# Projecting q one iteration earlier, the right sums in y's banks, and x1's column sums taken by ScalarE copies

## The reference, cut to what matters

```python
# layer 0: triangle multiplication
x = _layernorm(pair, ln1_w, ln1_b)
left = sigmoid(x @ left1) * (x @ left2)
right = sigmoid(x @ right1) * (x @ right2)
p = einsum('nsre,nkre->nske', left, right)
p = _layernorm(p, ln2_w, ln2_b)
x1 = pair + einsum('nrse,ez->nsrz', p, out_w) * sigmoid(x @ gate)
...
# layer 1
left = x1 @ W_left + b_left + x1 @ W_eq + b_eq
right_sum = sum(x1 @ W_right + b_right, axis=2, keepdims=True)
out = left * right_sum * sigmoid(x1 @ W_gate + b_gate)
return _layer_norm(out @ W_out + b_out + x1, ln_scale, ln_bias)
```

## Time and profile before

| what | value |
|---|---|
| median of 3 runs | 104.78 us (103.95 to 104.85) |
| the profiled execution, its own time | 103.82 us |
| its span, first to last instruction | 101.9 us |
| busy share of the span: TensorE, VectorE, ScalarE, GpSimd | 78%, 69%, 59%, 52% |
| mean granted TensorE clock | 0.958 |

### The profile page before, as it was taken

How to read it: one execution, slowest core, us unless ns; L and a number is a source line. 1 busy time by engine, 2 the same in 40 slices (tenths; PEclk the granted TensorE clock), 3 DMA queues, 4 the chain that set the end, 5 groups by cost and what they waited for, 6 DMA issues and landing times.

```text
span 101.9 us, 3186 instructions
## 1 busy us (share of the span) xinstructions
PE 79.4 (78%) x1260; PEld 59.5 (58%) x1260; DVE 70.5 (69%) x286; ACT 60.4 (59%) x101; POOL 52.9 (52%) x69
## 2 busy tenths in 40 slices
PE   0997999789999999998894889889898779750000
PEld 0994887667877899644552466757566467640000
DVE  0477697946466800399978799997979897299700
ACT  0643977998776267689259944895429762922000
POOL 5138994899910050008555454089075769946400
PEclk9999999999999999999999999999999999998555
DMA  3999997000000000000000000000000606447996
GB/s 50 193 152 147 144 146 77 13 10 13 0 0 6 3 0 0 0 0 0 0 6 3 3 0 6 0 6 0 6 0 6 103 12 98 66 66 115 145 145 97
DMA packets 34079, 4.68 MB, mean 46 GB/s; under 512 B 33936, under 2 KB 34064, under 8 KB 34064
## 3 DMA queue, kind: packets, MB, share of 16 engines
q1 hardware_dynamic: 32304, 4.10, 32.0%
q10 hardware_dynamic: 1760, 0.38, 2.0%
HBM read 2.38 MB, written 2.10 MB: 44 GB/s over the span
## 4 chain that ended last, share of the span: by engine, by line
PE 37%; DVE 29%; ACT 16%; issue 6%; POOL 5%; DVEq 1%; POOLq 0%
PE bank L831 10%; PE bank L894 7%; DVE x1T L709 7%; PE bank L904 5%; DVE stats L670 4%; PE bank L838 4%; PE bank L816 3%; ACT sig L524 3%; ACT L424 3%; DVE o_a L718 3%; DVE st L724 2%; POOL xc L306 2%; DVE lr L742 2%; DVE stats L591 2%; DVE lr L606 2%
## 5 line engine op out<-in xcount | busy, mean ns | idle before, releaser
L367 POOL TENSOR_TENSOR t_tok<-p_sb,rstd 128x512 f32<-128x512 f32 x7 | 10.2, 1457 | 16.6 <-DVE rstd L676 15.8
L831 PE MATMUL bank<-lr_blk,xnT 64*128 64x256 f32 x128 | 15.6, 388 | 0.7 <-ACT xnT L435 0.7
L606 DVE TENSOR_TENSOR lr<-bank,sig_lr 128x512 f32<-128x512 f32 x16 | 10.9, 683 | 6.4 <-ACT sig_lr L444 6.4
L831 PEld LDWEIGHTS bank<-lr_blk,xnT 64*128 64x128 f32 x128 | 11.8, 186 | 3.2 <-issue 1.2
L670 DVE BATCH_NORM_STATS2 stats<-p_sb 128x6 f32<-128x64 f32 x64 | 8.6, 216 | 6.9 <-ACT p_sb L488 6.9
L376 POOL TENSOR_TENSOR oT<-o_a,rsum 128x512 f32<-128x512 f32 x8 | 8.3, 1044 | 8.5 <-DVE o_a L718 8.5
L444 ACT ACTIVATE sig_lr<-bank 128x512 f32<-128x512 f32 x16 | 9.6, 597 | 3.3 <-PE bank L831 3.1
L591 DVE BATCH_NORM_STATS2 stats<-x_tok 128x6 f32<-128x64 f32 x64 | 8.9, 213 | 1.4 <-DMA x_tok<-in_x 1.3
L396 POOL TENSOR_TENSOR sq<-lr,row_rep 128x512 f32<-128x512 f32 x6 | 8.0, 1336 | 2.6 <-DVE lr L742 1.8
L709 DVE SCALAR_TENSOR_TENSOR x1T<-bank,w_rep,u 128x128 f32<-128x128 f32 x32 | 9.3, 347 | 0.1
L306 POOL TENSOR_TENSOR xc<-x_tok,stats 128x512 f32<-128x512 f32 (+1 forms) x8 | 8.1, 1012 | 1.8 <-DVE stats L591 1.8
(11 more groups left out here) (98 smaller groups left out, 169.7 us busy)
## 6 DMA issues: line engine op xcount, KB each, us to landing
x_tok<-in_x SPq DMA_DIRECT2D x14, 128.0 KB, 4.2
out<-sq SPq DMA_DIRECT2D x7, 256.0 KB, 4.0
x_tok<-in_x SPq DMA_DIRECT2D x3, 64.0 KB, 3.1
w_rep<-in_weights ACTq DMA_DIRECT2D x4, 45.1 KB, 3.2
out<-sq ACTq DMA_DIRECT2D x1, 128.0 KB, 3.2
out<-sq SPq DMA_DIRECT2D x1, 128.0 KB, 4.8
x_tok<-in_x ACTq DMA_DIRECT2D x1, 64.0 KB, 2.7
scale_rep<-in_rows SPq DMA_DIRECT2D x1, 64.0 KB, 8.8
```

What stands on the lines that cost most here:

```text
L367: nc.gpsimd.tensor_tensor(t_tok[:, c % 2], by_token(p_sb[:, :, s]), by_token(rstd[:, 1:2, s]).to_broadcast([P, SPC, CH]), ALU.mult).then_i ...
L606: nc.vector.tensor_tensor(lr[:, :, s].rearrange("p f (b q) -> p b f q", q=GRP), src[:, :, 2 * CH:4 * CH], sig_lr[:, j % 3].rearrange("p (b ...
L831: last = nc.tensor.matmul(dst, xnT[half, c, k * P:(k + 1) * P], lr_blk[half], start=True, stop=True, skip_group_check=True)
```

## The change

TensorE projects q of chunk i in its iteration i, where it did so for chunk i-1, and behind y instead of ahead of layer 1's projections. From chunk 1 on the right sums are written into the spare half of the banks Y and not of Q; since `evacuate_y(c)` and `sums_of_right(c+2)` then read the same banks, `project_sums` of chunk c (c > 1) gives the signal `y_ps` that `evacuate_y(c-2)` waits for, and `sums_of_right(c)` waits for that square (`ysq_ready`). VectorE makes x1 of chunks 1 to 7 in one operation of 512 columns without sums. ScalarE makes the sums: `sum_x1(c)`, four copies of 128 columns that accumulate, for each of the chunks 1 to 7. The groups of the roots and the places where they stand in the loops are changed as well, and so is the order of `gate0`.

```diff
-ROOTS2 = [(0, 2), (2, 4), (4, 6), (6, 8)]
+ROOTS2 = [(0, 2), (2, 5), (5, 8)]
-ROOTS3 = [(0, 1), (1, 4), (4, 5), (5, 6), (6, 7), (7, 8)]
-ROOT3_AT = {4: [0], 7: [1], 9: [2, 3]}
+ROOTS3 = [(0, 1), (1, 3), (3, 4), (4, 6), (6, 7), (7, 8)]
+ROOT3_AT = {5: [0], 7: [1], 8: [2], 9: [3]}
...
+            def sum_x1(c):
+                act.wait_ge(x1_ready, BLK * (c + 1))
+                for j in range(BLK):
+                    last = nc.scalar.activation(x1_again[:, c % 2, j * P:(j + 1) * P], x1T[:, c % 3, j * P:(j + 1) * P],
+                                                ACT.Copy, accum_out=x1_sum[:, c, j:j + 1])
+                last.then_inc(x1_summed, 1)
...
-                if i in ROOT3_AT and i < CHUNKS:
-                    nc.scalar.activation(scratch[:], eps[:], ACT.Sigmoid)
+                if i == 3 or i in ROOT3_AT and i <= CHUNKS:
+                    nc.scalar.activation(scratch[:, i:i + 1], eps[:], ACT.Sigmoid)
...
             def sums_of_right(c):
-                dve.wait_ge(rs_ps, c + 1)
-                if c + 1 < CHUNKS:
-                    dve.wait_ge(q_ps, c + 2)
+                if c < 2:
+                    dve.wait_ge(rs_ps, c + 1)
+                else:
+                    dve.wait_ge(ysq_ready, c - 1)
...
+                if c:
+                    nc.vector.scalar_tensor_tensor(out=x1T[:, c % 3], in0=bank[:, XT], scalar=vec("b_out"),
+                                                   in1=u[:, c % 2], op0=ALU.add, op1=ALU.add).then_inc(x1_ready, BLK)
+                    return
...
             def project_sums(c):
-                pe.wait_ge(x1_ready, BLK * (c + 1))
                 if c:
-                    pe.wait_ge(rs_ready, c)
+                    pe.wait_ge(x1_summed, c)
...
-                last.then_inc(rs_ps, 1)
+                last.then_inc(y_ps if c > 1 else rs_ps, 1)
```

More of the change, by code:

```diff
@@ L401, in _ @@
             for i in range(CHUNKS + 2):
-                if i + 2 < CHUNKS:
+                if i + 2 < CHUNKS and i != 3:
                     normalise2(i + 2)
+                for c in BIAS_FIRST.get(i, []):
+                    bias3(c)
                 if 0 <= i - 2 < CHUNKS:
                     times_right(i - 2)
+                if i == 3:
+                    normalise2(5)
                 for c in BIAS_AT.get(i, []):
                     bias3(c)
-            for c in (3, 5, 6):
+            for c in (5, 6):
                 bias3(c)
@@ L466, in _ @@
                 root1_of(b)
-            nc.scalar.activation(scratch[:], eps[:], ACT.Sigmoid)
+            nc.scalar.activation(scratch[:, 0:1], eps[:], ACT.Sigmoid)
             affine1(4)
@@ L538, in _ @@
                     root2_of(1)
-                    evacuate_tT(1)
-                    root2_of(2)
-                    evacuate_tT(2)
+                    nc.scalar.activation(scratch[:, 1:2], eps[:], ACT.Sigmoid)
+                if i < CHUNKS:
+                    evacuate_tT(i)
+                if i == 1:
+                    gate0(2)
+                    gate0(6)
                 if i == 2:
-                    gate0(2)
-                    gate0(3)
                     act.wait_ge(biases, 3)
@@ L547, in _ @@
                     gate1(i - 2)
-                if i < CHUNKS and i not in (1, 2):
-                    evacuate_tT(i)
                 if i == 2:
-                    for c in range(4, CHUNKS):
+                    gate0(7)
+                if 0 < i - 1 < CHUNKS:
+                    sum_x1(i - 1)
+                if i == 2:
+                    for c in (3, 4, 5):
                         gate0(c)
-                if i == 4:
-                    root2_of(3)
+                if i == 3:
+                    root2_of(2)
                 if i == CHUNKS + 1:
@@ L690, in sums_of_right @@
             def sums_of_right(c):
[L691 to L694 removed]
+                if c < 2:
+                    dve.wait_ge(rs_ps, c + 1)
+                else:
+                    dve.wait_ge(ysq_ready, c - 1)
+                if c == 0:
+                    dve.wait_ge(q_ps, 2)
+                b = sums_bank(c)
+                nc.vector.tensor_scalar(two(rsum[:, c]), bank[:, b:b + 2, HALF:HALF + 2], right_bias[:], None, ALU.add
                                         ).then_inc(rs_ready, 1)
@@ L1040, in _ @@
             transpose_t(0)
[L1041 to L1047, removed]
+            project_q(0)
+            project_gate0(6)
+            transpose_t(1)
+            project_gate0(7)
+            project_sums(0)
+            project_q(1)
+            transpose_x(1)
+            for i in range(2, CHUNKS + 3):
+                if i < CHUNKS:
+                    transpose_t(i)
                 if 0 <= i - 2 < CHUNKS:
                     project_1(i - 2)
[L1050 to L1054, removed]
                 if 0 <= i - 3 < CHUNKS:
```

62 lines of the change are left out of this document (38 added, 24 removed).

## The result

| | before | after |
|---|---|---|
| median of the runs | 104.37 us (103.95 to 104.85, 4 runs) | 108.10 us (108.00 to 108.21, 4 runs) |
| the profiled execution, its own time | 103.82 us | 108.14 us |
| its span | 101.9 us | 106.3 us |
| mean granted TensorE clock | 0.958 | 0.936 |

The changed kernel is slower: ratio 1.0356, 95% interval 1.0294 to 1.0417. The forecast was 108.8, in a range from 105.5 to 112.0. The runs of the kernel before lie near 103.8 us or, with a mean granted clock of 0.944 to 0.948 instead of 0.953 to 0.965, near 104.8, so a median of a few of them depends on how many of either it holds.

A forecast was written before the change was run, and what follows sets the result against it. VectorE and TensorE waiting on each other bound the kernel, 4.48 us per x1; the change puts ScalarE's queue in that ring. Lag +1.0 in the opening, +4.9 at i = 8, +4.0 at the end: 104.8 + 4.0 = 108.8, range 105.5 to 112.0.

The forecast's parts named there:

- ScalarE's queue: ScalarE's copies, table loads, roots and squares in order; outside the wait cycle before, forecast to stand in it after the change.
- the ring: Cycle of waits from x1 to x1: VectorE and TensorE before, 4.48 us; after, through ScalarE's sums, TensorE and the square.
- a, the step of an accumulating copy: Start to start of ScalarE's 128-column accumulating copies: taken at 0.31 us, so 1.24 us a chunk, 28 copies in the path.
- The loads cost their row: Each ScalarE table load costs 1.30 us to the next start, not the skill page's 2.66 per switch.
- Opening, x1(3) at 64.8: ScalarE full until layer 0's last root at 61.1; x1 of chunk 3 at 64.8 instead of 63.78, +1.0.
- i = 4 to 8: Loop iterations followed through ScalarE's queue: lag +0.6 at x1(4), +1.5 at x1(6), +1.9 at x1(7), +4.9 at `o_a(7)`.
- End: root over at 93.15, tail "the same work": Root for chunks 4 and 5 ends at 93.15 instead of 89.16; VectorE's tail behind it unchanged, so end 4.0 later.
- The sum: Whole effect: +4.0 us on the profiled execution, 107.8; with the median 0.96 above that execution, 108.8.
- Cheap copies: First rival: fixed step and read-out hidden, a = 0.12, sum falls by 5.3 to -1.3, 103.5; chance 0.07.
- a free read-out: Second rival: the copies' read-out costs nothing, a = 0.20, +0.9, 105.7, about no change; chance 0.14.
- dear copies: Third rival: a = 0.40 gives +6.5, 111.3; a = 0.49 gives +9.0, 113.8; chance 0.09.
- The fourth: Rival: q still waits for x1, `u` starts 0.5 late, time stays 108.8; chance within the forecast's 0.70.

The follow-up runs named there:

- run 1: Changed kernel with x1's sums back on VectorE in four operations, no ScalarE copies, eleven loads kept: 103.14 us, ratio 0.9877 to the kernel before.
- run 5: Kernel before with only x1 in one VectorE operation and its sums by ScalarE copies, seven loads: 108.02 us, ratio 1.0419.
- run 6: Changed kernel with one accumulating copy of 512 columns per chunk instead of four of 128 (sums not the reference's): 105.19 us, ratio 1.0125.
- run 7: Changed kernel with chunk 3's root joined to the group at i = 7, nine loads instead of eleven: 107.22 us, ratio 1.0326.
- run 4: Changed kernel with 16 further identity products on TensorE filling gaps in the last iterations: 108.08 us, ratio 1.0353.
- run 8: Changed kernel with x1's sums back on VectorE and nine loads (edits of run 1 and run 7): 103.13 us, ratio 0.9923.
- run 9: run 8's kernel with GpSimd's products with the right sums moved ahead of the scales and biases: 104.25 us, ratio 0.9997 to the kernel before.
- run 10: Kernel before with the output of chunks 0 to 5 not stored, two stores instead of eight: 102.97 us.
- run 11: run 1's kernel with the output of chunks 0 to 5 not stored, two stores instead of eight: 101.75 us.
- run 2: Changed kernel with the last norm's roots in fewer groups, seven loads instead of eleven, sums still on ScalarE: 108.22 us, ratio 1.0366.
- run 3: Changed kernel with sums back on VectorE and seven loads (edits of run 1 and run 2): 105.59 us, ratio 1.0107.

## Why the prediction was right, step by step

- **ScalarE's queue comes into the ring.** Right, and shown: taking the copies out turns the loss into a gain (run 1), putting them alone into the kernel before gives the whole loss, there in the old order (run 5), making them shorter takes most of it back (run 6). The chain names the same lines.
- **a, the step of an accumulating copy.** Taken at 0.31, measured 0.29. The read-out is a row of its own of 0.19, but the next copy starts 0.09 behind its start (79.76 to 79.85), which goes with the 0.20 estimated for a copy of 128 columns. 28 copies make that 28 x 0.02 = 0.6 us too much. Small steps elsewhere took most of it back by the end of the loop, such as that from the square to x1 (83.78 - 82.36 = 1.42, taken at 1.37); that they did is luck.
- **The loads cost their row.** Right: eleven loads, each of 1.28 us, and after one the next instruction started within 0.02. The Trainium skill, page "ScalarE: Activation LUTs", section "What ACT_TABLE_LOAD costs", puts a switch at 2.66 us; here the measurement decides, and run 7 took two loads away for 1.2 us on the path. That is less than the two rows (2.6), since TensorE then came last.
- **Opening, x1(3) at 64.8.** Measured 64.77. The reciprocal waited 2.02 us for the root, as the step said:

```profile
62.98 0.45 DVE L701 RECIPROCAL rstd<-std 128x48 f32<-128x48 f32 x1 [2.02 <-ACT std L437]
```

- **i = 4 to 8.** x1(4) forecast at 68.9, measured 69.02; x1(6) 78.7 and 78.77; x1(7) 83.7 and 83.78; `o_a(7)` 90.55 and 90.48. In the earlier trace rows the last stood at 85.67, so the lag there is 4.8, as forecast (4.9). Run 7 puts the two loads of iteration 8 at 1.2 or more of it.
- **End: root over at 93.15, tail "the same work".** Both halves were wrong, and cancelled to 0.3. The root was over at 94.35, 1.2 late, because TensorE ran at half clock from 86 us on, which the forecast had taken to be at full speed as it was at this place before; run 4 shows that these 1.2 us are the clock's. And the tail behind it, from the reciprocal to VectorE's end, was 1.0 shorter (6.38 instead of 7.37): in the timeline of the changed kernel one step of VectorE takes 0.69, since the GpSimd operation ahead of it has just ended (94.70),

```profile
93.43 1.27 POOL L405 TENSOR_TENSOR sq<-lr,row_rep 128x512 f32<-128x512 f32 x1
...
94.76 0.69 DVE L775 TENSOR_TENSOR lr<-lr,rstd 128x512 f32<-128x512 f32 x1
```

and in that of the kernel before it took 1.70, since GpSimd's operation began only 0.12 us ahead of it:

```profile
89.24 1.27 POOL L396 TENSOR_TENSOR sq<-lr,row_rep 128x512 f32<-128x512 f32 x1
...
89.36 1.70 DVE L742 TENSOR_TENSOR lr<-lr,rstd 128x512 f32<-128x512 f32 x1
```

The two errors hang together. In run 4 the root came earlier against x1, and yet the step ended 0.55 behind GpSimd's operation (96.01 against 95.46); in the changed kernel it ended 0.75 behind it (95.45 against 94.70). So the earlier root gained next to nothing, and that the fallen clock left the end where the forecast had put it is luck.

- **The sum.** +4.0 was forecast on the profiled execution, +4.3 measured (108.14 - 103.82). The forecast of 108.8 lies 0.7 above the median all the same: it took over the 0.96 by which the median of three runs of before lay above its profiled execution, and the changed kernel's median lies 0.04 below its own. So the 0.7 comes from the base and not from the mechanism.
- **The rivals.** Cheap copies (a = 0.12), a free read-out (0.20) and dear copies (0.40) fall with a = 0.29. The fourth falls too: q is really ahead, for `u` starts without a wait; its gain is only visible with the sums on VectorE.

What is left of the change without the copies is faster than the kernel before: with x1 left as it was, it gives 0.9877 (run 1) or 0.9923 (run 8). The two intervals overlap, so which version is better stays open. In the loop VectorE's wait for q is gone, and in quiet iterations x1 follows x1 in 4.05 us instead of 4.48. But q ahead and the sums in y's banks were not tested alone: the regrouped roots of layer 0's second norm and the order of `gate0` stayed in all these runs, and of the lead of 2.7 us at x1(7) 1.5 is there at x1(3). What of it the opening gives stays open.

Run 1's kernel keeps 1.0 us of the 2.7 in its span. That the two loads of iteration 8 take the larger part of what is lost is read from its rows; runs 8 and 9 removed them, but each let another delay in on GpSimd, so it is not shown by a time. The stores take another part (runs 10 and 11).

## What to carry to other kernels

An engine with idle time is not a free place for work: its idle time lies beside its own queue, and work that others wait for drags the whole queue (here loads, roots and squares) into the ring. Before moving a reduction to another engine, take its step from start to start, multiply by the copies on the path, and ask which later instruction of the ring it stands ahead of. And a gain in the loop is not one at the end: look at what the earlier end then runs beside, since in runs 2, 3, 4 and 9 an earlier end of the loop was paid back in the tail or the stores.

## What the runs showed of the hardware

- A VectorE operation on two SBUF tiles that starts after a GpSimd one has begun ends about 0.55 us after that one's end: in the kernel before at 91.06 against 90.51, in run 4 at 96.01 against 95.46, in run 9 at 89.11 against 88.55. So it took from 0.97 (run 1, at 87.95) to 1.75 us instead of 0.68, and a shift of a few tenths of a microsecond decides. The other way round, a GpSimd operation that began at 96.72 in the changed kernel, 0.16 behind a VectorE one, took 1.64 instead of 1.27. The Trainium skill, page "SBUF — State Buffer", section "Who interferes with whom", says that a VectorE instruction with two SBUF inputs contends with a GpSimd one that reads SBUF, and that the order of issue decides who blocks; these rows agree.
- TensorE's granted clock fell to 0.50 (1.2 GHz) in the loop, at about 85.9 us in the changed kernel, in the second of two gaps of 1.64 and 0.85 us (82.28 to 83.92 and 85.40 to 86.25) with 1.4 us of products between, and was at 1.00 again in 93 to 94 us. Sixteen small products in the gaps kept it at 1.00.
- ScalarE's read-out of an accumulated sum is a row of 0.19, but the next copy starts 0.09 behind its start, and the step from copy to copy of 128 columns is 0.29.
- Output transfers that ran beside nothing else went at 144 to 146 GB/s, with the DMA engines busy for 0.94 to 0.96 of the time (runs 1 and 3, 96 to 100 us), and set the end of the span: from VectorE's end to the span's it was 4.9 us with two stores and 5.5 to 7.9 with eight.
